# A one-core language tower: the first group's step sizes spread and its convolution done by TensorE products

## The reference

```python
proj = x @ in_proj_w.T
zgate, u, Bc, Cc, dt = jnp.split(proj, [DIN, 2 * DIN, 2 * DIN + N_, 2 * DIN + 2 * N_], axis=-1)
xBC = causal depthwise convolution of [u, Bc, Cc], 4 taps, plus conv_b
xBC = jax.nn.silu(xBC)
Bc = Bc * rsqrt(sum(Bc * Bc) + 1e-06); Cc likewise
dt = softplus(dt + dt_bias)
# scan over the 128 positions, for 8 heads of 64 and 16 states
z = (z + d * (B u - A * y)) / (1.0 + d * d * A);  y = y + d * z;  out = y . C
yout = (out + D_skip * u) * silu(zgate);  return yout @ out_proj_w.T + out_proj_b
```

## Time and profile before

| | us |
|---|---|
| median of 3 runs (lowest, highest) | 1299.3 (1297.9, 1300.29) |
| the profiled execution, its own time | 1299.55 |
| its span in the profile | 1297.7 |
| PE busy | 1157.6 (89%) |
| DVE busy | 1099.3 (85%) |
| ACT busy | 793.0 (61%) |
| POOL busy | 708.0 (55%) |

### The profile page before, as it was taken

How to read it: one execution, slowest core, us unless ns; L and a number is a source line. 1 busy time by engine, 2 the same in 40 slices (tenths; PEclk the granted TensorE clock), 3 DMA queues, 4 the chain that set the end, 5 groups by cost and what they waited for, 6 DMA issues and landing times. The chain is left out here.

```text
span 1297.7 us, 25052 instructions
## 1 busy us (share of the span) xinstructions
PE 1157.6 (89%) x7309; PEld 763.4 (59%) x7316; DVE 1099.3 (85%) x1980; ACT 793.0 (61%) x1275; POOL 708.0 (55%) x2062
## 2 busy tenths in 40 slices
PE   2991075999999999999999999999999999999986
PEld 1550032557575767666666667675767576667554
DVE  5998989979888988888888888888989897877188
ACT  4666757384848484748475756657574747452367
POOL 8882010748485757575757575757576665640000
PEclk9999997899999999999999999999999999999989
DMA  9999901010101010101010000000000101000015
GB/s 356 407 408 417 398 22 35 1 36 1 36 1 37 2 35 1 34 2 33 7 28 12 23 17 18 18 17 19 16 24 11 34 1 35 2 19 1 1 66 194
DMA packets 37137, 91.60 MB, mean 71 GB/s; under 512 B 10141, under 2 KB 21746, under 8 KB 32738
## 3 DMA queue, kind: packets, MB, share of 16 engines
q1 hardware_dynamic: 33442, 81.32, 17.8%
q0 software_dynamic: 3072, 8.39, 1.7%
q10 hardware_dynamic: 576, 1.31, 0.3%
HBM read 81.29 MB, written 9.70 MB: 70 GB/s over the span
## 5 line engine op out<-in xcount | busy, mean ns | idle before, releaser
L802 POOL TENSOR_TENSOR stp<-Gs,X 128x32 f32<-128x32 f32 x900 | 263.3, 293 | 253.3 <-ACT X L775 186.3
L804 POOL TENSOR_TENSOR Gs<-Gs,stp 128x32 f32<-128x32 f32 x900 | 270.6, 301 | 70.5
L1203 PE MATMUL bank<-w_fc,gl 128*128 128x256 f32 x1024 | 246.6, 384 | 5.4 <-ACT gl L1194 5.4
L1184 PE MATMUL bank<-mT,w_fc 128*128 128x512 f32 x512 | 236.7, 595 | 1.5 <-ACT mT L1164 1.5
L1203 PEld LDWEIGHTS bank<-w_fc,gl 128*128 128x128 f32 x1024 | 190.4, 191 | 70.7 <-issue 29.8
L652 PE MATMUL bank<-xT,w_in 128*128 128x512 f32 x448 | 207.2, 603 | 4.3 <-DVE uT L1097 4.1
L964 ACT ACTIVATE uT<-bank,cols 128x512 f32<-128x512 f32 x64 | 47.9, 776 | 219.8 <-DVE sz L1104 161.3
L1184 PEld LDWEIGHTS bank<-mT,w_fc 128*128 128x128 f32 x512 | 94.9, 190 | 85.5 <-issue 79.7
L978 DVE SCALAR_TENSOR_TENSOR uT<-bank,cols,uT 128x500 f32<-128x500 f32 (+1 forms) x192 | 133.4, 735 | 2.3
L652 PEld LDWEIGHTS bank<-xT,w_in 128*128 128x128 f32 x448 | 81.8, 191 | 88.3 <-issue 77.8
L358 DVE TENSOR_TENSOR peak<-ring,peak 128x1536 f32<-128x1536 f32 (+2 forms) x67 | 115.3, 1721 | 9.2 <-ACT ring L257 6.9
(11 more groups left out here) (219 smaller groups left out, 1887.9 us busy)
## 6 DMA issues: line engine op xcount, KB each, us to landing
ring<-in_table SPq DMA_DIRECT2D x31, 1536.0 KB
d_rep<-d_rows SPq DMA_DIRECT2D x128, 64.0 KB, 2.0
out<-res SPq DMA_DIRECT2D x16, 512.0 KB, 2.9
b_rep<-bc_rows SPq DMA_DIRECT2D x128, 32.0 KB, 1.8
c_rep<-bc_rows SPq DMA_DIRECT2D x128, 32.0 KB, 1.8
w_fc<-in_w_fc SPq DMA_DIRECT2D x2, 1024.0 KB, 15.0
ring<-in_table SPq DMA_DIRECT2D x2, 768.0 KB
w_in<-in_w_in ACTq DMA_DIRECT2D x1, 1088.0 KB
```

What stands on the lines that cost most here:

```text
L802: pool.tensor_tensor(stp[:], Gs[:, t, ::-1, :], X2[:, t, :, :], ALU.mult).then_inc(rec.sem, 1)
L804: pool.tensor_tensor(Gs[:, t + 1, :, :], Gs[:, t, :, :], stp[:], ALU.add).then_inc(rec.sem, 1)
L1184: last = pe.matmul(pj[n % 4][:, :], w_fc1[:, k, n * P:(n + 1) * P], mT[:, k, :], start=(k == 0), stop=(k == KD - 1))
L1203: last = pe.matmul(sbk[j // 2][:, (j % 2) * D:(j % 2 + 1) * D], gl[n % LEAD][:, j * LEN:(j + 1) * LEN], w_fc2[:, n, :], start=False, stop= ...
```

## The change

Only turns 0 and 1 change. The replicated step sizes of the first group no longer come from DRAM: PE multiplies `dd` by constant matrices (`head_of`, loaded into `gl`, which are free then) into the two banks `sbk`, and ACT scales from there into X. The stores and loads of `sp_replicate` for that group stay, but X doesn't wait for them. The u convolution of the first group is done by PE, as four accumulating products for each tile with diagonal matrices of the taps (`u_diag`, loaded into `MT`); ACT copies raw u to `uT` first, and applies bias and silu from the banks afterwards. z of the first group goes to the banks `sbk` instead of `pj`. `dve_bc` of the first group and `dve_conv_small` of the second move into `dve_first_products`. ACT's lists for turns 0 and 1 are written out, the first warming loses eight of twelve products, and six loads of 256 KB are issued by SP at the start of the block.

```diff
+        def pe_spread_d(pe):
+            pe.wait_ge(first_in, 16 * (TAPS + HG))
+            pe.wait_ge(d_ready.sem, d_ready.at(0))
+            for hg in range(HG):
+                for j in range(G):
+                    last = pe.matmul(sbk[hg][:, j * LEN:(j + 1) * LEN], gl[hg][:, j * P:(j + 1) * P], dd[:],
+                                     start=True, stop=True)
+            last.then_inc(d_spread, 1)
+
+        def act_rep_first(act):
+            act.wait_ge(d_spread, 1)
+            for hg in range(HG):
+                for part, w in ((0, "omega"), (1, "neg_omega")):
+                    act.activation(X2[:, :, part, hg * SC:(hg + 1) * SC], chunks(sbk[hg][:, :]), ACT.Copy,
+                                   scale=c(w, hg)).then_inc(x_ready.sem, 1)
...
@@ dve_first_products, behind the products of fours and eights
+            dve_bc(dve, 0)
@@ dve_first_products, ahead of the two last steps
+            dve_conv_small(dve, 1)
...
+        def act_u_raw(act):
+            for f in range(UT):
+                act.wait_ge(u_mm.sem, u_mm.at(0, f + 1))
+                act.activation(uT[:, f, :], pj[f][:, :], ACT.Copy).then_inc(u_tap0.sem, 1)
+
+        def pe_conv_u(pe):
+            for f in range(UT):
+                pe.wait_ge(u_tap0.sem, u_tap0.at(0, f + 1))
+                dst = pj[f][:, :].rearrange("p (s t) -> p s t", s=G)
+                src = uT[:, f, :].rearrange("p (s t) -> p s t", s=G)
+                for i in range(TAPS):
+                    last = pe.matmul(dst[:, :, i:], MT[TAPS - 1 - i][:, f, :], src[:, :, 0:LEN - i], start=(i == 0),
+                                     stop=(i == TAPS - 1), skip_group_check=True)
+                last.then_inc(u_cv.sem, TAPS - 1)
+
+        def act_silu_first(act):
+            for f in range(UT):
+                act.wait_ge(u_cv.sem, u_cv.at(0, (f + 1) * (TAPS - 1)))
+                act.activation(uT[:, f, :], pj[f][:, :], ACT.Silu, bias=c("u_bias", f)).then_inc(u_ready.sem, 1)
...
+        def z_bank(g, f):
+            return sbk[f % 2] if isinstance(g, int) and g == 0 else pj[f]
+
         def pe_z(pe, g, f):
-            pe.wait_ge(u_cv.sem, u_cv.at(g, u_convolved(f)))
+            if since(g):
+                pe.wait_ge(u_cv.sem, u_cv.at(g, u_convolved(f)))
+            elif f < 2:
+                pe.wait_ge(x_ready.sem, x_ready.at(0, 2 * f + 2))
+            else:
+                pe.wait_ge(z_ready.sem, z_ready.at(0, f - 1))
...
@@ pe_turn
                 if first:
                     pe_small(pe, g)
+                if second and not third:
+                    pe_conv_u(pe)
                 if first and not second:
                     pe_u(pe, g, (0, 1))
+                    pe_spread_d(pe)
...
-                            pe_warm(pe, sbk[0], 12)
+                            pe_warm(pe, sbk[0], 4)
...
@@ act_turn
+            def first_turn():
+                act_rows_T(act, 0)
+                act_small_in(act, 0)
+                act_small_dt(act, 0)
+                act_small_silu(act, 0)
+                act_rep_first(act)
+                act_u_raw(act)
+                act_silu_z(act, 0, (0, 1))
+                act_small_norm(act, 0)
+                act.preload_act_table_set("natural_log_exp_and_others")
+                act_small_rsqrt(act, 0)
+                act_norm_rows(act, 1)
+
+            def second_turn():
+                act_rows_T(act, 1)
+                act_small_in(act, 1)
+                act_small_dt(act, 1)
+                act_silu_z(act, 0, (2, 3))
+                act_small_silu(act, 1)
+                act_small_norm(act, 1)
+                act.preload_act_table_set("natural_log_exp_and_others")
+                act_small_rsqrt(act, 1)
+                act_squares(act, 0)
+                act_rep(act, 1, (0, 1))
+                act_silu_first(act)
+                act_layer_norm(act, 0)
+                act_utok(act, 0)
+                act_u_tap0(act, 1)
+                act_norm_rows(act, 2)
...
@@ dve_turn
-                if first:
+                if first and not filling:
                     dve_conv_small(dve, g)
...
-                    dve_conv_u(dve, g, (0, 1))
-                    dve_bc(dve, g)
-                    dve_conv_u(dve, g, (2,))
-                    dve_conv_u(dve, g, (3,))
                     dve_first_products(dve)
...
@@ sync engine, start of the block
                 sp.dma_start(utok[:, 0, 0:D], a["out_b"]).then_inc(bias_in, 16)
+                for i in range(TAPS):
+                    sp.dma_start(MT[i][:], a["u_diag"][:, i, :, :]).then_inc(first_in, 16)
+                for hg in range(HG):
+                    sp.dma_start(gl[hg][:], a["head_of"][:, hg, :]).then_inc(first_in, 16)
```

More of the change, by code:

```diff
@@ L475, in build @@
         begun = sem("begun")
+        first_in = sem("first_in")
+        d_spread = sem("d_spread")
         bias_in, halved, pick_cleared = sem("bias_in"), sem("halved"), sem("pick_cleared")
@@ L990, in act_silu_u @@
                 act.activation(uT[:, f, :], uT[:, f, :], ACT.Silu).then_inc(u_ready.sem, 1)
+        def z_bank(g, f):
+            return sbk[f % 2] if isinstance(g, int) and g == 0 else pj[f]
         def pe_z(pe, g, f):
-            pe.wait_ge(u_cv.sem, u_cv.at(g, u_convolved(f)))
+            if since(g):
[4 more added lines that the diff above has]
+                pe.wait_ge(z_ready.sem, z_ready.at(0, f - 1))
             if f < UT - 1:
-                project(pe, pj[f][:, :], f * P, (f + 1) * P, z_mm.sem)
+                project(pe, z_bank(g, f)[:, :], f * P, (f + 1) * P, z_mm.sem)
                 return
             for k in range(KD):
-                last = pe.matmul(pj[f][:, :], w_in[:, k, f * P:(f + 1) * P], xT[:, k, :],
+                last = pe.matmul(z_bank(g, f)[:, :], w_in[:, k, f * P:(f + 1) * P], xT[:, k, :],
                                  start=(k == 0), stop=(k == KD - 1))
@@ L1010, in act_silu_z @@
                 act.wait_ge(z_mm.sem, z_mm.at(g, f + 1))
-                act.activation(sz[:, f, :], pj[f][:, :], ACT.Silu).then_inc(z_ready.sem, 1)
+                act.activation(sz[:, f, :], z_bank(g, f)[:, :], ACT.Silu).then_inc(z_ready.sem, 1)
         def pe_u_T(pe, g, staged, j):
@@ L1370, in act_turn @@
         def act_turn(act):
-            def turn(g, first, second, third, fourth, nxt):
+            def first_turn():
[26 more added lines that the diff above has]
+                act_norm_rows(act, 2)
+                act_silu_u(act, 1, (0, 1))
+                act_silu_u(act, 1, (2,))
+                act_sum_squares(act, 0, 0)
+                act_silu_u(act, 1, (3,))
+                act_sum_squares(act, 0, 1)
+            def turn(g, first, second, third, fourth, nxt):
+                if first and not third:
+                    if second:
+                        second_turn()
+                    else:
+                        first_turn()
+                    return
                 p, m = g - 1, g - 2
@@ L1393, in turn @@
                     act_small_rsqrt(act, g)
[L1394 to L1403, removed]
                 if fourth and third and not second:
@@ L1867 @@
     s, t = np.arange(P)[:, None, None], np.arange(LEN).reshape(1, CH, CL)
+    diagonals = np.zeros((P, TAPS, UT, P), np.float32)
+    for i in range(TAPS):
+        for ft in range(UT):
+            np.fill_diagonal(diagonals[:, i, ft, :], taps[ft * P:(ft + 1) * P, i])
+    head_of = np.zeros((P, HG, G, P), np.float32)
+    for hg in range(HG):
+        for j in range(G):
+            head_of[SMALL * j + 4 * hg + np.arange(P) // 32, hg, j, np.arange(P)] = 1.0
+    head_of = head_of.reshape(P, HG, G * P)
     ids = x.astype(np.int32) if x.dtype != np.int32 else x
@@ L1885 @@
         "fc2_b": rows(f["L0_attn_fc2_b"]),
+        "u_diag": diagonals,
+        "head_of": head_of,
         "q_cols": np.stack([tall(f["L0_ffn_weight_scale"]), tall(f["L0_ffn_bias"])], axis=1),
```

## The result

| | before | changed |
|---|---|---|
| median (lowest to highest), 7 runs each | 1299.3 (1297.9 to 1302.19) | 1304.71 (1303.12 to 1306.34) |
| span of the profiled execution | 1297.7 | 1302.8 |
| PE / DVE / ACT busy | 1157.6 / 1099.3 / 793.0 | 1162.3 / 1089.0 / 789.6 |

The changed kernel is slower: ratio 1.0043, 95% interval 1.0034 to 1.0052, or 4.4 to 6.8 us. DVE has 10 us less to do and ACT 3, PE 5 more; the time follows none of these but the chain of waits in turn 1.

What follows compares the result with a forecast made beforehand. PE fills the thirteen periods; the edit shifts the first scan product at 241.91, behind scores where query and token chains meet. 1299.55 + 7.0 (5.9 chain, 1.1 half clock) = 1306.5 us; range 1302.5 to 1311.3.

Steps and rivals of the forecast that it cites:

- The deciding step: PE, turn 1: 13.7 us of u convolution ahead of group 1's square sums, ACT queued behind; first scan product 5.9 us later.
- The spread: Turn 0: PE's eight products 2.1 us, ACT's four activations 4.4; X of group 0 ready at 192.2, 5.0 us earlier.
- Constants: Six loads of constants (1.5 MB) near 169 take 4 us, hidden until 185.3; nothing taken.
- The periods: Between 274 and 1092 us: thirteen periods filled by PE, 62.9 or 63.0 us each, still 62.95 after the edit.
- DVE: Turn 1: keys' first step at 212.5, 3.0 us gained, which ends in 9 us of idling before the masks.
- The clock: Half clock in second z tiles, first warming, scores and second warming: 1.1 us for all, 7.0 us in sum.
- The end: Behind 241.91 the orders are unchanged, so the shift is carried to the end: 1299.55 + 7.0 = 1306.5 us.
- The first: Scores of group 0: DVE's chain stays the bound, at most 3.9 us faster, 1296.1; 6%.
- The second: Absorbed within 0.2%: PE at full clock all through, 3.3 us, and 0.7 or more saved in hops; 1302.1 and less; 6%.
- The third: First warming wholly at half clock, scores and second warming as before: 11.8 us, 1311.3; 14%.
- The fourth: u convolution: a product costs one record's time, 6.9 us in all; scan product 0.8 us later, 1300.3; 1%.
- The drain: ACT, behind table loads: by the skill page two switches would add 2.8 us, sum 1309.3; not taken.

Runs made afterwards that it cites:

- The first experiment: Changed kernel with L713 moved between the second and third tile of the u convolution: 1300.84 us, ratio 1.0003 to the kernel before.
- The reordered kernel: Changed kernel, all work kept, with PE's convolution tiles and L713 and ACT's turn 1 list put in another order: 1292.5 us, ratio 0.9941 to the kernel before.
- experiment 5: Not a run number: the text means by experiment, 5 to 7 us. Run meant: the reordered kernel without the spread, 1298.27 us, ratio 0.9995.

## Why the prediction was right

**The deciding step.** It put L713 at 221.7 to 222.0 behind the convolution, and it ran at 222.21. From there each hop came within 0.9 us of its place: squares 224.87 to 226.8 (226.3), X of group 1 until 231.0 (230.7), u silu until 234.7 (234.1), scores 243.04 (242.4), masks 245.11 (244.5), scan product 248.62 (247.8). ACT's idle time of 8.02 us and DVE's of 8.23 are those foretold. The first experiment shows the cause and not the order of events alone: moving L713 by itself took 5.0 us back at the scan product and 6.7 us at the scores.

**The spread.** PE's part was 2.02 us where 2.1 was taken. The four activations into X took 2.42 us where I took 4.40, "the strided write being the same": that reason was wrong. The write wasn't what cost; reading the same strided pattern from PSUM went at almost twice the speed, and the lower bound of 2.2 would have been the value to take. An idle DVE wasn't the reason, since X took 4.37 us from SBUF while DVE stood idle (the kernel without the spread, from 194.05). The faster X changed nothing at the end, since PE came to z only behind u and ACT waited for it (0.60 and 0.60 us of silu behind pauses of 1.0 and 1.1).

**Constants.** Six loads were issued by 171.9, and the spread started 0.14 us after the step sizes were there. Nothing was paid.

**The periods.** I had the period of the loop wrong, without effect on the sum. The windows of 62.95 us that I laid over it are not its period: in both kernels the same row (the scaled rows' transposes, L1157 and L1207) comes again every 62.7 us in the steady turns.

**DVE.** Keys began at 212.92 (212.5 forecast) and the sum of squares waited 2.39 us (2.1 forecast). X came 1.5 us earlier than forecast, and lost it to waits of 0.65 us for the norm factors and 2.08 us for group 1's small projections. The gain ended in that wait and in the idle 8.23 us, as written.

**The clock.** I took 1.1 us for all half-clock terms. The sum at the scan product, 6.7 us, has 0.8 us that come from half clock ahead of anything edited (the step sizes were ready at 186.11, not 185.34; other kernels with the same six loads had them at 185.2 to 185.6). Without it the sum is 5.9 us, what the chain gave before any term for the clock. So 7.0 came near 6.7 partly by luck. The first warming took 4.85 us, 0.4 more than forecast, and scores and second warming ran at full clock.

**The end.** "The shift is carried to the end" held until 1185 us and then lost 1.6 us to a fall of the clock in the profiled execution of the kernel before. That is why the sum, right to 0.3 us where it was worked out, lies 1.8 us above the median. What a span carries on top of its chain is the clock of that one execution, and the step should have had a term of 1 to 2 us either way for it. How much of the 5.4 us between the medians is such clock isn't shown, as only one execution of each kernel has a trace.

**The rivals.** The first (DVE's chain stays the bound) needed the u silu 12.4 us earlier. The reordered kernel brought it 14.2 us earlier (220.5 against 234.7), and there the rival's mechanism did hold, with 1292.5, and more than the 3.9 us I had allowed. My bound of 3.9 counted a lead of 3.0 us at the keys, and there it was 5.7 (209.84 against 215.51): X from PSUM was 2.0 us faster than I took, and the wait for the small taps was gone. The shorter wait behind the second warming came on top. (Its time was also added wrongly: 1299.55 less 3.9 is 1295.65, not 1296.1.) The second wanted full clock all through, and the transposes at 200.24 took 1.97 us, at half clock. The third wanted the first warming wholly at half clock (6.8 us) and half clock in scores and second warming; they took 4.85, 2.01 and 3.70 us. The fourth, that a product takes one record's time, fell: 16 products, 32 records, 13.84 us, 0.43 us each. The Trainium skill ("TensorE: Matmul & The Clock Gate", "Back-to-back issue gap") has 216 ns for 512 columns and no word there on float32; in this case a float32 product of 512 columns took two records of twice that. The drain that the Trainium skill ("ScalarE: Activation LUTs", "What ACT_TABLE_LOAD costs") puts behind a table load didn't show: the load at 231.00 took 1.28 us and the silu started at 232.30.

## What to carry to other kernels

Where queues are written out by hand, price an added block of work by what stands behind it in the queue: here a product of 0.38 us, needed by another engine, stood behind 13.8 us of products that nobody was waiting for yet. A step that is made faster is worth nothing until its consumer is what others wait for: by the waits the spread was worth nothing in one order, and by experiment 5 to 7 us in the other. Judge warming products by whether PE would wait at that place anyway: between the links of a late chain they cost time (3.2 us here), and where PE would wait anyway they paid (scores in 2.01 us, not 3.69). Before you read a gain from two traces, compare a row ahead of the edit: here these rows lay up to 1.4 us apart.

## What the runs showed of the hardware

- Four activations of 128x512 into X took 2.42 us when they read PSUM and 4.3 to 4.5 us when they read the same pattern from SBUF; the writes were the same, and DVE was idle in one case of either.
- The clock came back to full while PE did nothing but transposes: 16 of them, from 234.72, and the scores at 239.85 ran at full clock. In another kernel 16 transposes with a pause of 2.84 us between them did not bring it back. With a single tile of convolution (3.56 us) ahead of the first transposes of turn 1 and 1.48 us of idle time left behind it, the transposes took 1.09 us, at full clock; with the same tile and 4.77 us of idle time (the kernel without the spread) they took 1.97.
- The same kernel's executions differ by 2 to 8 us. A fall of the clock in the last scan turn, a place that no edit touches, stands in six of eleven traces and was worth 1.6 us in one and 3.2 in another. A claim on 2 us of this kernel from one pair of traces would not stand.
